# A transformer attention layer on one core: the moments of the residual are taken one slot later, and two small DVE tensors are laid out in every other word

## The reference: what is computed

```
q, k = x @ Wq.T, x @ Wk.T ;  v = x @ Wv.T + bv
scores = q k^T * 384**-0.5 + (adj + adj)          # per head, 128 x 128
row_nonzero = any(scores != 0, axis=-1)           # a row of zeros gives a row of zeros
p = softmax(where(row_nonzero, scores, -inf)), NaN -> 0
att = p v                                         # heads side by side, 128 x 384
y = x + att @ Wo.T + bo
out = (y - mean(y)) / sqrt(var(y) + 1e-5)         # over the 384 channels
```

## Time and profile before

| | before |
|---|---|
| median of 3 executions | 638.47 us (637.63 to 639.18) |
| profiled execution, its own time | 637.14 us |
| its span, first to last instruction | 635.4 us |
| mean granted clock of PE | 0.993 |
| PE busy | 593.0 us, 93% |
| DVE busy | 482.7 us, 76% |
| ACT busy | 497.6 us, 78% |
| POOL busy | 452.6 us, 71% |

### The profile page before, as it was taken

One profiled execution on the slowest core, in us unless ns is written; L12 is line 12 of the kernel. 1 busy time (PEld: TensorE's weight loads), 2 busy tenths in 40 slices (PEclk: granted clock), 3 DMA queues, 4 the chain that ended last, 5 costly groups with the idle time before them and its releaser, 6 DMA issues.

```text
span 635.4 us, 23731 instructions
## 1 busy us (share of the span) xinstructions
PE 593.0 (93%) x8448; PEld 518.5 (82%) x8448; DVE 482.7 (76%) x2380; ACT 497.6 (78%) x1975; POOL 452.6 (71%) x691
## 2 busy tenths in 40 slices
PE   8899999999999999999999999999999999999773
PEld 5788888888888888888888888888878888888663
DVE  4778877877877877877877877777887787787884
ACT  5688778778788778778878877877878878877882
POOL 1577777777687687778768678777768768667773
PEclk9999999999999999999999999999999999999998
DMA  8311324232142422224242132423214222112221
GB/s 305 134 37 46 109 85 137 75 110 84 47 134 87 125 84 64 95 82 135 84 126 81 39 121 86 132 80 91 91 58 135 86 75 86 52 52 86 87 79 50
DMA packets 34749, 59.63 MB, mean 94 GB/s; under 512 B 10568, under 2 KB 24008, under 8 KB 34632
## 3 DMA queue, kind: packets, MB, share of 16 engines
q1 hardware_dynamic: 34200, 57.53, 28.1%
q10 hardware_dynamic: 432, 0.59, 0.3%
HBM read 44.50 MB, written 13.62 MB: 91 GB/s over the span
## 4 chain that ended last, share of the span: by engine, by line
PE 74%; DVE 19%; issue 3%; DMA 3%; ACT 0%; POOLq 0%; POOL 0%; DVEq 0%
PE qk_ps L339 32%; PE scores_ps L430 16%; PE v_ps L373 15%; PE scores_ps L360 9%; DVE y L639 6%; DVE stats L642 5%; DVE att_n L626 5%; DMA scale_t<-scale_mem 2%; PE scores_ps L442 1%; DMA scale_mem<-scale_rows 1%; DMA x_raw<-xt 1%; DVE nscores L558 1%; DVE mean_var L644 0%; PE v_ps L442 0%; PE qk_ps L442 0%
## 5 line engine op out<-in xcount | busy, mean ns | idle before, releaser
L473 ACT ACTIVATE probs<-nscores,neg_max 128x128 f32<-128x128 f32 x768 | 297.5, 389 | 34.7 <-DVE neg_max L558 34.7
L287 POOL TENSOR_TENSOR tree<-nscores 128x512 f32<-128x512 f32 (+1 forms) x128 | 143.1, 1118 | 115.1 <-DVE neg_max L558 115.1
L558 DVE CUSTOM_DVE_ANT_0 nscores<-scores_ps,adj_n 128x128 f32<-128x128 f32 x768 | 171.9, 286 | 4.0 <-PE scores_ps L360 1.7
L473 ACT ACTIVATION_READ_ACCUMULATOR probs<-nscores,neg_max 128x1 f32 x768 | 144.0, 187 | 0.0
L287 POOL TENSOR_TENSOR tree<-tree 128x128 f32<-128x128 f32 (+2 forms) x256 | 127.8, 499 | 20.1
L639 DVE TENSOR_TENSOR y<-scores_ps,x_n 128x384 f32<-128x384 f32 x64 | 35.7, 558 | 110.2 <-PE scores_ps L430 110.2
L430 PE MATMUL scores_ps<-w_o,att_t 128*128 128x384 f32 x576 | 112.8, 341 | 7.1 <-DVE att_t L630 4.6
L373 PE MATMUL v_ps<-w_v,x_t 128*128 128x384 f32 x576 | 111.7, 338 | 1.1 <-ACT probs_t L498 1.1
L339 PE MATMUL qk_ps<-x_t,w_k 128*128 128x512 f32 (+1 forms) x540 | 108.9, 346 | 0.0
L373 PEld LDWEIGHTS v_ps<-w_v,x_t 128*128 128x128 f32 x576 | 102.2, 188 | 7.4 <-ACT probs_t L498 1.9
L339 PE MATMUL qk_ps<-x_t,w_q 128*128 128x512 f32 (+1 forms) x540 | 107.5, 343 | 0.0
(11 more groups left out here) (71 smaller groups left out, 928.0 us busy)
## 6 DMA issues: line engine op xcount, KB each, us to landing
x_n<-xn SPq DMA_DIRECT2D x32, 384.0 KB, 4.8
scale_t<-scale_mem SPq DMA_DIRECT2D x63, 192.0 KB
out<-out_n SPq DMA_DIRECT2D x31, 384.0 KB, 2.6
x_raw<-xt SPq DMA_DIRECT2D x15, 768.0 KB, 5.4
adj_n<-adj SPq DMA_DIRECT2D x32, 128.0 KB, 4.4
scale_mem<-scale_rows SPq DMA_DIRECT2D x63, 16.0 KB
x_raw<-xt SPq DMA_DIRECT2D x3, 256.0 KB, 4.8
nscores<-wq ACTq DMA_DIRECT2D x3, 192.0 KB, 4.2
```

Of the source, the lines that this page charges most:

```text
L287: nc.gpsimd.tensor_tensor(tree[:, b % 2, low:high, 0:width], src[:, :, 0:width], src[:, :, width:2 * width], ALU.add).then_inc(tree_step, 1)
L473: last = nc.scalar.activation(probs[:, b % 2, h], nscores[:, b % 2, h], ACT.Exp, bias=neg_max[:, b % 2, h:h + 1], scale=-1.0, accum_out=ro ...
L558: last = nc.vector.tensor_tensor_reduce(out=nscores[:, half, h], in0=scores_ps[j][:, m * P:(m + 1) * P], in1=adj_n[:, b // 2 % 2, half], s ...
```

## The change

Two edits. In the first, the two instructions that find the moments leave `residual` and become a function of their own, `moments`. For block b - 2 they are now issued in slot b, after the maxima of the first four heads of block b + 1; before, they were issued at the end of slot b - 1, right behind `y` of that block and ahead of `normalise`. At the end of the kernel they stand where they stood. In the second, `total` and `nonzero` get a buffer of twice the size and use every other float of it, so that each of their 12 values is 8 bytes from the next.

```
-        total = sb("total", [P, HEADS])
-        nonzero = sb("nonzero", [P, HEADS])
+        total = sb("total", [P, HEADS, 2])[:, :, 0]
+        nonzero = sb("nonzero", [P, HEADS, 2])[:, :, 0]
...
                 nc.vector.tensor_tensor(y[:, half], out_bank(b)[:, 0:HID], x_n[:, b // 2 % 2, half],
                                         ALU.add).then_inc(y_ready, 1)
+
+            def moments(b):
+                half = b % 2
                 dve.wait_ge(y_ready, b + 1)
                 nc.vector.bn_stats(stats[:], y[:, half]).then_inc(stats_done, 1)
                 dve.wait_ge(stats_done, b + 1)
...
                 if has(b + 1):
                     bias_and_max(b + 1, 0)
+                if has(b - 2) and has(b):
+                    moments(b - 2)
+                if has(b + 1):
                     bias_and_max(b + 1, 1)
                 if has(b - 1):
                     attention_low(b - 1)
...
                 elif b == NB:
                     residual(b - 2)
+                    moments(b - 2)
                     residual(b - 1)
+                    moments(b - 1)
             normalised_last(NB - 1)
```

More of the change, by code:

```diff
@@ L588, in find_scale @@
                 dve.wait_ge(tree_step, STEPS * (b + 1))
-                nc.vector.reduce_sum(total[:], tree[:, half, :, 0:REST], axis=mybir.AxisListType.X).then_inc(total_done, 1)
+                nc.vector.reduce_sum(total, tree[:, half, :, 0:REST], axis=mybir.AxisListType.X).then_inc(total_done, 1)
                 dve.wait_ge(total_done, b + 1)
-                nc.vector.scalar_tensor_tensor(out=nonzero[:], in0=neg_max[:, half], scalar=0.0, in1=total[:],
+                nc.vector.scalar_tensor_tensor(out=nonzero, in0=neg_max[:, half], scalar=0.0, in1=total,
                                                op0=ALU.not_equal, op1=ALU.max).then_inc(nonzero_done, 1)
@@ L601, in find_scale @@
                         out=scale_n[:].rearrange("p (h d) -> p h d", h=HEADS),
-                        in0=nonzero[:].unsqueeze(2).to_broadcast([P, HEADS, D]), scalar=0.0,
+                        in0=nonzero.unsqueeze(2).to_broadcast([P, HEADS, D]), scalar=0.0,
                         in1=recip[:].unsqueeze(2).to_broadcast([P, HEADS, D]),
@@ L608, in find_scale @@
                 nc.vector.scalar_tensor_tensor(out=row_scale[:, 0:HEADS].rearrange("p (j m) -> p m j", m=KT),
-                                               in0=nonzero[:].rearrange("p (m j) -> p m j", m=KT), scalar=0.0,
+                                               in0=nonzero.rearrange("p (m j) -> p m j", m=KT), scalar=0.0,
                                                in1=recip[:].rearrange("p (m j) -> p m j", m=KT),
```

## The result

| | before | after |
|---|---|---|
| median | 638.05 us (636.72 to 639.18, 4 runs) | 651.99 us (650.98 to 653.55, 4 runs) |
| profiled execution's span | 635.4 us | 650.3 us |
| PE / DVE busy | 593.0 / 482.7 us | 605.0 / 529.2 us |
| ACT / POOL busy | 497.6 / 452.6 us | 497.8 / 445.9 us |

The ratio is 1.0221 (95% interval 1.0192 to 1.0251). The forecast was 620.5 us with a range to 650.5: the time is above the range.

A forecast was written before the change was run, and what follows sets the result against it. PE was taken as the bound, waiting each slot for `att_n` behind DVE's moments. 637.14 - 18.8 + 1.0 (DMAs) = 619.3, or 620.6 beside the median, said as 620.5; range 615.5 to 650.5.

The forecast's parts named there:

- no hold: Slots with projections: with every-other-word tensors, DVE's `nonzero` and `row_scale` do not wait for long POOL operations; chance 0.48.
- The rival of the hold: DVE's `nonzero` and `row_scale` wait for POOL's L275 and L268: +9 us, so 647; in full 0.35, at 641 to 652.
- the two loops: Under held `row_scale`: DVE with POOL, 9.77 us with L268, 9.14 without; the scale's way through DRAM, 9.65.
- the tail: From slot 59 on, without projections, the moments were to cost the same wherever they stand: nothing gained.
- The gain: Slots 2 to 58, moments out of the chain before `att_n`: 0.33 us per slot, bounds 0.20 and 0.51, sum 18.8.
- The scale's DMAs: `att_n` waiting for `scale_t` through DRAM: 1 us expected in all; as second rival 6 us, time 626, chance 0.07.
- the costs of the move itself: Copies and later DVE maxima come 0.35 us later, hidden before `y`; the step of two costs 0.6 us at most.

The follow-up runs named there:

- e1: The first edit alone on the kernel before, `total` and `nonzero` left in adjacent words: 652.45 us, ratio 1.0224.
- e2: The second edit alone on the kernel before, moments where they were: 638.01 us, ratio 0.9998.
- e7: The full change, but POOL writes zeros instead of computing the low half of later x (L268), reading nothing of SBUF: 623.36 us, ratio 0.9753.
- e10: The full change, with the moments again right behind `y` from slot 58 on: 647.41 us, ratio 1.0147.
- e9: As e5, but from slot 58 on the moments stand again right behind `y`: 613.88 us, ratio 0.9615.
- e5: First edit, adjacent words, with POOL's L268 one slot later, at its slot's start once the scale's rows are turned: 620.67 us, ratio 0.972.
- e3: The full change, but `nonzero` lies in free columns of a PSUM bank in all slots but the last: 631.90 us, ratio 0.992.

## Why the prediction was wrong

**The step that failed is edit 2.** "I take no hold, at little better than evens": the hold stayed, with and without the step (e1, e2). The prediction had the evidence on its table and argued it away. `scale_n`, with a step of 0 on both inputs, had held POOL off, and no row at all showed a two-input instruction that went free under a POOL operation. More of it lay in the trace before: L268 held 6 of the 64 `nonzero`, up to 1.28 us, and 36 others started in its last 0.03 to 0.18 us, too late to lose anything by it. The prediction's slot is one of these: its `nonzero` starts 0.06 before L268 ends, so the two do meet, and only the end of the wait lies within the 0.17 us that `nonzero` takes anyway. The rule of the Trainium skill, "SBUF — State Buffer", section "Who interferes with whom", makes no exception for steps; the trace of the change agrees with it (1.0 us at a step of two), and e7 agrees with its other half, that a GpSimd instruction that only writes does not contend. But not every POOL operation that reads SBUF holds DVE to its end: under `rstd` (L298), one column wide, 19 of the 63 `row_scale` of the kernel before took 0.21 us at the most, and the one below ended 0.34 us ahead of it. What sets that apart was not tested.

```profile
217.80 0.55 POOL L298 TENSOR_TENSOR rstd<-var_eps,minus_half 128x1 f32<-128x1 f32 x1
217.80 0.21 DVE L608 SCALAR_TENSOR_TENSOR row_scale<-nonzero,recip 128x12 f32<-128x12 f32 x1
```

The lean to "no hold" rested on the difference between one word read again and a word skipped, which nothing supported.

**The rival of the hold** was right in place and mechanism: `row_scale` of about 1 us behind L268, `nonzero` behind L275, `att_n` waiting for `scale_t`, sometimes `total` for the tree. Its price for the 57 slots, +9, was measured as +9.2 (7.1 in e1, 9.3 in e10). By line the chain gives the scale's DMAs 24% and 11% and POOL's tree 12%: the two loops that I had set side by side, DVE with POOL and the way through DRAM, take turns.

**The term that no case had is the tail.** "From slot 59 on [...] the moments cost the same wherever they stand": they cost 6.2 us more. Before, they stood between `y` and `att_n`, beside `attend` on PE. Moved, they stand ahead of `attention_low`, which `project_out` waits for, and `attend` is queued behind `project_out`. I had counted DVE's sum and not who waits behind it. PE now idles for 1.80 to 2.24 us before the four `project_out` from 600 to 629 us, where it was 1.15 to 1.19, and its granted clock falls to 0.84 of full speed from 610 to 630 us. The nine products that took 1.83 us take 3.04, 2.65, 2.21 and 2.20 in the last four steps: 2.8 of the 6.2 us. The first of them in the chain:

```profile
609.22 3.04 PE scores_ps L430 x9
612.26 1.08 PE scores_ps L413 x24
```

The moments also delay `find_rstd` and the tree, and e9 and e10 bring these forward too, so they alone do not part the two causes. The chain does: in the change it has nothing of POOL between 592 and 646 us. In e5 it does pass through the tree, at 581 to 585 us and at 590 to 594 us, so there a part of the tail is the late tree's. This is what put the time above the range: 647 and 6 is 653. e9 and e10 give 6.8 and 4.6 for it, with other differences between executions in both; the last five steps take 38.2 to 40.2 us in the five profiles with the old order and 42.6 to 45.5 in the seven with the new one.

**The gain was under-sized.** I took 0.33 per slot, between bounds of 0.20 and 0.51; with no hold it is 9.46 - 9.00 = 0.46. The gap behind `turn` closes to nothing (e5): the 0.22 between `attend` and `turn` was no model for it. The whole gain of e9, 23.7 us, is near 57 x 0.46 = 26 less what the DMAs take. That e5 came out at the forecast's 620.5 is two errors that cancel in part, and luck. In its profiled execution (623.87 us) the 57 slots take 521.25 us, where the forecast had 521.7 with its 1 us for the DMAs: a slot of 9.00 instead of 9.14 makes up for 8.3 us of late slots instead of 1. The tail's 6.9 us more stood in no sum, and the profiled execution is 4.6 us above the 619.3 that the prediction had for it; only the median of the four comes near 620.5.

**The scale's DMAs** bind in single slots, as said; 1 us was too little, 8.3 us of e5 lie over its slots of 9.00, 6.2 of them in slots with a wait for `scale_t` and 1.5 in the one slot behind the longest wait, where the granted clock was low. Right were the costs of the move itself: the three copies and the maxima stayed hidden, with DVE idle for 1.15 us before `y` (1.2 predicted), and the step cost nothing.

## What to carry to other kernels

Before an instruction is moved, lay its new time over the other engine that shares its reads: in the kernel before, `nonzero` came into the last 0.18 us of a 1.3 us POOL operation in 36 slots and lost nothing, and a shift of half a microsecond cost more than it gained. The cure was to move the long operation into time in which its engine waits anyway, not to change the layout. And look at the last slots by themselves: where a stage falls away, another queue has become the path, and what was hidden isn't.

## What the runs showed of the hardware

- A DVE `scalar_tensor_tensor` with two inputs in SBUF waits to the end of POOL's 128x384 and 128x512 operations that read SBUF, 0.03 us beyond it, at a step of one (1.01 us in e1) and of two (1.00 in the change); in one row with a step of zero POOL was the one held. It takes 0.17 us under a POOL operation that only writes (e7), and 0.18 with one input in PSUM (e3). Under the 128x1 operation of L298 it took 0.21 us at the most (kernel before).
- PE's granted clock fell after idle times of 1.61 us (e5, before 264.92), 2.24 (the change, before 609.22) and 2.43 (e5, before 599.80). It did not fall after 1.15 to 1.19 us in the tail before, nor after 1.84 in the change (before 600.23), but it did after 1.14 in e7 (before 541.11): the length of the last idle time alone does not decide. Nine products took 2.80 us against 1.83, so a late wait can be paid twice.
- The switch from the transposes of `turn` to the products of `score` costs PE's weight loads no gap when all waits are fulfilled (e5), while `attend` to `turn` shows 0.2 us in every kernel here.
